# The window-attention stage written out without a loop, its context transposes moved from its first steps to its last, and the expert weights of a routed layer prepared by GpSimd alone

## The reference, cut to what matters

```python
x = x + L0_xattn(layernorm(x), ctx, ...)     # 64 channels, 8 heads of 8, sliding window of 16 along the 512 positions
x = x + L0_ffn(layernorm(x), Wg, Wu, Wd, ...)
x = x + L1_xattn(layernorm(x), ctx, ctx, pos, mask, Wq, Wk, Wv, Wo)     # 32 heads, 8 key heads, width 128
logits = x_norm @ gate_w                      # L1_ffn: routed, 8 experts, the best 2 of each token
w = softmax(top2(logits))
x = x + sum over the 2 experts of w * (x_norm @ expert_w[e])
```

## Time and profile before

| | us |
|---|---|
| median of 3 runs | 1152.22 |
| lowest, highest of them | 1150.52, 1155.11 |
| the profiled execution, its own time | 1149.5 |
| its span in the trace | 1147.7 |
| busy within the span: PE, DVE, POOL, ACT | 1034.4, 662.4, 486.7, 391.5 |

### The profile page before, as it was taken

How to read it: one execution, slowest core, us unless ns; L and a number is a source line. 1 busy time by engine, 2 the same in 40 slices (tenths; PEclk the granted TensorE clock), 3 DMA queues, 4 the chain that set the end, 5 groups by cost and what they waited for, 6 DMA issues and landing times. The chain is left out here.

```text
span 1147.7 us, 24031 instructions
## 1 busy us (share of the span) xinstructions
PE 1034.4 (90%) x9074; PEld 853.3 (74%) x9074; DVE 662.4 (58%) x1380; ACT 391.5 (34%) x894; POOL 486.7 (42%) x539
## 2 busy tenths in 40 slices
PE   6787787999999889999999999999999999754894
PEld 3565566788888678888888888888888888533783
DVE  3787786454454576566565666556566565850424
ACT  3776874222222333222222232222222221511431
POOL 0443442341213245445444455544445542134755
PEclk8898999999999979999999999999999999985997
DMA  7000002655543021111101111110010100035778
GB/s 243 12 3 4 3 4 58 238 179 217 183 174 103 19 74 38 47 29 28 56 29 48 29 28 47 34 51 29 28 47 29 37 10 1 0 119 174 252 237 271
DMA packets 51803, 92.08 MB, mean 80 GB/s; under 512 B 10744, under 2 KB 24312, under 8 KB 51256
## 3 DMA queue, kind: packets, MB, share of 16 engines
q1 hardware_dynamic: 42104, 69.13, 19.0%
q10 hardware_dynamic: 6624, 12.06, 3.1%
q0 software_dynamic: 2976, 9.44, 2.5%
HBM read 77.25 MB, written 36.18 MB: 99 GB/s over the span
## 5 line engine op out<-in xcount | busy, mean ns | idle before, releaser
L115 PE MATMUL PS<-NTh,W 128*128 128x256 f32 (+2 forms) x688 | 216.6, 315 | 0.0
L116 PE MATMUL PS<-NTl,W 128*128 128x256 f32 (+2 forms) x688 | 214.1, 311 | 0.4 <-issue 0.2
L117 PE MATMUL PS<-NTh,W 128*128 128x256 f32 (+2 forms) x688 | 213.9, 311 | 0.0
L116 PEld LDWEIGHTS PS<-NTl,W 128*128 128x128 f32 (+1 forms) x688 | 131.4, 191 | 7.6 <-issue 0.8
L117 PEld LDWEIGHTS PS<-NTh,W 128*128 128x128 f32 (+1 forms) x688 | 129.4, 188 | 8.4
L115 PEld LDWEIGHTS PS<-NTh,W 128*128 128x128 f32 (+1 forms) x688 | 129.7, 188 | 7.1
L1437 POOL TENSOR_TENSOR W<-ca_raw,W 128x512 fp32r<-128x512 f32 x64 | 82.7, 1294 | 115.1 <-ACT W L1287 115.1
L1375 DVE TENSOR_REDUCE ca_su<-room 128x4 f32<-128x256 f32 x64 | 26.9, 420 | 155.8 <-ACT room L1303 155.8
L1404 DVE TENSOR_TENSOR room<-PS,ca_sinT 64x512 f32<-64x512 f32 (+1 forms) x192 | 115.0, 599 | 2.6
L115 PE MATMUL PS<-W,ca_aTh 128*128 128x512 f32 x256 | 106.3, 415 | 3.5 <-DVE X L1392 3.5
L1303 ACT ACTIVATE room<-room 128x256 f32<-128x256 f32 x64 | 26.8, 418 | 222.8 <-POOL room L1484 222.8
(11 more groups left out here) (241 smaller groups left out, 2336.5 us busy)
## 6 DMA issues: line engine op xcount, KB each, us to landing
ca_raw<-in_L_Wq SPq DMA_DIRECT2D x32, 256.0 KB, 2.7
ca_raw<-in_L_Wo SPq DMA_DIRECT2D x32, 256.0 KB, 2.6
rf_raw<-in_experts SPq DMA_DIRECT2D x28, 256.0 KB, 4.0
room<-slots ACTq DMA_DIRECT2D x23, 256.0 KB, 3.4
outs<-room ACTq DMA_DIRECT2D x23, 256.0 KB, 3.8
outs<-blank SPq DMA_DIRECT2D x11, 512.0 KB, 9.0
room<-in_L_Wg SPq DMA_DIRECT2D x10, 256.0 KB, 2.7
room<-in_L_Wu SPq DMA_DIRECT2D x10, 256.0 KB, 3.0
```

The source lines that it names most:

```text
L115: nc.tensor.matmul(out, l_hi, r_hi, start=first, stop=False)
L116: nc.tensor.matmul(out, l_hi, r_lo, start=False, stop=False)
L117: return nc.tensor.matmul(out, l_lo, r_hi, start=False, stop=last)
```

## The change

`pipeline` is no longer called in the first stage. Each engine runs `unrolled`, which writes out all steps n = -4 to 37. The context tiles are transposed by a new piece at the end of steps 32 to 35, two tiles in a step, through PSUM banks 0 and 1, in which the scores were. It waits until the scores of all 32 units have been read out. Two waits are added: PE waits itself for the load of the context before the k projection of tile 0 and of tile 2, and ACT waits at n = 0 until its own masked copies of q are done. One wait (`ct_lo` at TT, before the first L471) is dropped. In the last stage ACT no longer makes high parts in its steps 1 to 4; POOL makes those of experts 2 to 7.

```diff
+def unrolled(eng, step, begin, end, body, per):
+    for n in range(begin, end):
+        step(n, n % body, n // per)
...
-    STEPS = (-4, 8, 24, UNITS + 6, 8, UNITS_PER_TILE)
+    STEPS = (-4, UNITS + 6, 8, UNITS_PER_TILE)
...
-        CT = [sh.PS[:, 2, :], sh.PS[:, 3, :]]
+        CT = [sh.PS[:, 0, :], sh.PS[:, 1, :]]
...
+        def context_due(n):
+            first = 2 * (n - UNITS) if isinstance(n, int) else -1
+            return range(first, first + 2) if 0 <= first < TT else ()
...
@@ tensor
                 def project_context(t, which, done):
+                    if isinstance(t, int) and t in (0, FIRST):
+                        pe.wait_ge(ctx_loaded[t], 16)
...
-                    c = n + 4
-                    if isinstance(n, int) and c < TT:
-                        pe.wait_ge(ctx_loaded[c], 16)
-                        if c >= 2:
-                            pe.wait_ge(S["ct_lo"], c - 1)
-                        for k in range(EC):
-                            last = nc.tensor.transpose(CT[c % 2][:, k * P:(k + 1) * P], sh.CTX[:, c, k * P:(k + 1) * P], ident)
-                        last.then_inc(S["ct_tr"], 1)
...
-                        else:
-                            pe.wait_ge(S["ct_lo"], TT)
...
-                pipeline(pe, step, *STEPS)
+                    for c in context_due(n):
+                        if c == 0:
+                            pe.wait_ge(S["keyed"], UNITS)
+                        if c >= 2:
+                            pe.wait_ge(S["ct_lo"], c - 1)
+                        for k in range(EC):
+                            last = nc.tensor.transpose(CT[c % 2][:, k * P:(k + 1) * P], sh.CTX[:, c, k * P:(k + 1) * P], ident)
+                        last.then_inc(S["ct_tr"], 1)
+
+                unrolled(pe, step, *STEPS)
@@ scalar
                         if q == 0:
+                            if isinstance(t, int) and t == 0:
+                                act.wait_ge(S["q_ready"], 1)
                             add_bias(t + 1, 0, "q_mm", qp[:], "q_biased")
@@ routed_ffn, scalar
-                    if 1 <= j <= 4:
-                        expert_high(2 + (j - 1) // 2, range((j - 1) % 2 * 2, (j - 1) % 2 * 2 + 2))
@@ routed_ffn, gpsimd
-                for e in (1, 2, 3):
-                    expert_low(e)
-                for e in range(RING, EXPERTS):
-                    gp.wait_ge(S["planned"], 1)
-                    done = gp.value_load(free_at[0:1, e - RING:e - RING + 1], min_val=1, max_val=SLOT_TILES + 1)
-                    gp.wait_ge(S["d_mm"], done)
-                    gp.sem_inc(S["planned"])
+                expert_low(1)
+                for e in range(2, EXPERTS):
+                    if e >= RING:
+                        gp.wait_ge(S["planned"], 1)
+                        done = gp.value_load(free_at[0:1, e - RING:e - RING + 1], min_val=1, max_val=SLOT_TILES + 1)
+                        gp.wait_ge(S["d_mm"], done)
+                        gp.sem_inc(S["planned"])
                     for p in range(EC):
```

More of the change, by code:

```diff
@@ L565, in step @@
                                                 sh.CTh[:, :, tok].bitcast(F32), ALU.subtract).then_inc(S["ct_lo"], 1)
-                pipeline(vec, step, *STEPS)
+                unrolled(vec, step, *STEPS)
             @block.gpsimd
@@ L596, in step @@
                                                 ALU.mult).then_inc(S["probs"], 1)
-                pipeline(gp, step, *STEPS)
+                unrolled(gp, step, *STEPS)
             @block.scalar
@@ L669, in step @@
                                              ACT.Copy).then_inc(S["ct_hi"], 1)
-                pipeline(act, step, *STEPS)
+                unrolled(act, step, *STEPS)
         return range(min(x.num for x in S.values()), max(x.num for x in S.values()) + 1)
@@ L1667, in _, with expert_high @@
             def _(act):
-                def expert_high(e, chunks=range(EC)):
-                    for p in chunks:
+                def expert_high(e):
+                    for p in range(EC):
                         k = e * EC + p
```

## The result

The change is faster. Its median is 1142.94 us (8 runs, 1138.53 to 1145.68) against 1153.56 for the kernel before (8 runs, 1150.52 to 1157.72): ratio 0.9904, 95% interval 0.9887 to 0.9920. In a later comparison (six runs) it was 0.9911, 0.9886 to 0.9936. The prediction said 1143.7. The profiled execution took 1139.67 us against 1149.5, a difference of 9.8, and its span is 1137.8. The first stage ends 11.4 us earlier (191.33 and 179.92), and 1.5 us of that are lost again behind it.

The account below looks back on a forecast made before the run. PE is busy 1034.4 of 1147.7 us; gains lie where it waits, in the first stage and first routed tiles. Terms -4.6 - 2.4 - 4.7 - 0.9 + 5.1 - 1.0 = -8.5 take 1152.2 to 1143.7 us; range 1136.5 to 1150.

Parts of the forecast that it names:

- rival 4: Start and routed layer: both gains at full size, -9 and -3; sum -12.5 us, 1139.7 us; chance 0.10.
- the sign of being right: End of the first stage: the last addition to X, at 190.98 us before, would come at 183.5.
- Start, -4.6: Up to unit 0's score read-out: without context work DVE reads out at about 27.2 us, not 31.85; -4.6 us.
- rival 1: First 45 us: PE pauses more, stays at half clock, start gives 3 us only; sum -4.5, 1147.7 us; chance 0.20.
- Unit 0 to 4, -2.4: Read-outs of units 0 to 4: half of 6.7 us context work saved, 0.9 lost to the clock; -2.4 us.
- Loop, -4.7 and -0.9: First-stage loop written out: -4.7 us for one branch back, -0.9 us for shorter waits at three tile boundaries.
- Rival 2: First stage: written-out code must be fetched, four PE pauses of 4.7 us; sum +10.3, 1162.5 us; chance 0.06.
- Tail, +5.1: End of first stage: context work adds 3.9 us over three steps, the end moves 191.33 to 196.4; +5.1 us.
- The ring: Last steps of 3.07 us: ACT's two high parts between its output and values copies lengthen each by 1.3 us.
- Routed layer, -1.0: First slot tiles: the wait behind ACT's weight chunks goes, third tile starts 1.1 us earlier, less 0.1; -1.0 us.
- Rival 3: Routed layer: POOL holds DVE's small tables throughout; sum -6.2 us, 1146.0 us; chance 0.12.
- the 3 us that the prediction gave as a sign: PE: no pause of over 3 us with the releaser "issue" if the prediction is right.

Follow-up runs that it names:

- e4: The kernel before with only PE's first-stage steps written out, DVE, ACT and POOL keeping their loop; 1146.80 us, ratio 0.9947.
- e5: The kernel before with DVE, ACT and POOL written out in the first stage and PE keeping its loop; 1152.62 us, ratio 1.0009.
- e10: The change with context work moved within its steps on PE and ACT, not on DVE, and DVE's routing tables spread over three slot tiles; 1137.68 us, ratio 0.9879.
- e3: The kernel before with only the experts' weight part of the change; 1148.05 us, ratio 0.9972.
- e6: The change with the context work moved to other places within the same last steps on PE, ACT and DVE; 1139.00 us, ratio 0.9889.
- e2: The kernel before, loop kept, with only the context transposes moved to steps 32 to 35 and the two added waits; 1146.16 us, ratio 0.9952.
- e9: The kernel before, context tiles left in front, with DVE's statistics of tiles 2 to 7 made earlier and one ACT wait added; 1146.36 us, ratio 0.9973.
- e1: The kernel before with the first stage written out on all four engines and nothing else changed; 1146.42 us, ratio 0.9954.

## Why the prediction was right, and where its steps were off

The sum was -8.5 us. In the first comparison the medians differ by 10.6 and the profiled executions by 9.8, in the second the medians by 10.0. The sign, the places and the size hold; no rival decided it. That the total came so close is in part luck. The first stage gained 11.4 us where the terms that lie in it sum to 7.5: the start with units 0 to 4 gave 8.3, nearer to rival 4's 9 than to the 7.0 taken, and the tail cost 2 less. Then 3.2 us, for which the sum had nothing, went the other way behind it. The last addition to X came at 179.58, below the 183.5 given as the sign of being right. The terms one by one:

- **Start, -4.6: measured -3.8, and -4.0 over all executions.** The mechanism is as said: DVE is no longer late, and ACT's last copy is next. The step that failed is the time of that copy, 24.8 in the prediction and 25.96 in the profile. Of these 1.2, 0.5 were there from the start (the first projection begins at 14.33 in place of 13.84, chance by the other executions; counted from it the term is -4.3); 0.4 are ACT's wait of 0.33 for the v projection at half clock, with the 0.1 by which operations in a row overlap; 0.2 are the two context copies, counted at 0.59 where the next operation had followed at 0.48. The mask and the scores then took 1.8 at half clock, 0.5 more than the prediction's 1.3 and 0.75 more than the 1.08 that they take at full clock (before, from 37.47), but the slack given was larger. So the clock's part, rival 1's mechanism in the place that it named, is 0.4 + 0.75, some 1.2 us, where rival 1 had 4.
- **Unit 0 to 4, -2.4: measured -4.5, and -4.1 over all.** Two parts. The work was put at half of 6.7, which was too little; the clock had the wrong sign. I added 0.9 for a PE that would pause more. In fact before has half clock at 44 to 48, and after full clock from 30 on. The four operations of PE from 43.80 to 49.04 before take 1.9 us longer than the same ones in after at full clock (L378 2.05 for 1.13, L426 0.77 for 0.49, L433 1.10 for 0.67, L471 1.09 for 0.85), and that is about the most that the clock gave: the other half clock of before in these steps, at 32 to 36 (0.61 and 0.54), has its like in after at 28 to 30. In e4, with the context tiles in place, PE has full clock from 40 us on, and unit 0 to 4 takes 15.64 against 16.04 to 16.53 in the other four, so there it was worth 0.4 to 0.9. The rest of the 4.1 is DVE's and ACT's work and waits. Before, PE fell at 42 to 44 behind 2.1 us of idle time that the context tiles caused; without the delay there was no such pause. By these rows the delays, not the transposes, set the clock here; no run took out one without the other.
- **Loop, -4.7 and -0.9: measured -6.0, and -5.7 over all.** Right in mechanism, and by e4 and e5 narrower than stated: PE's branch alone, with the transfer of code in its pause. The Trainium skill's page "Runtime: NRT & Kernel Launch" (section "Instruction fetch mechanics") holds that straight code is fetched ahead and that a taken branch can make the engine wait for its code. The trace agrees, with the transfer of 16 KB in the pause of 3.60. Rival 2 (pauses of 4.7 us in the written-out code) did not come: the longest pause of that kind in the first stage is 0.9. Why three engines pass their branch without a loss no run here shows. Nor was it tested that a constant in place of a register is what shortens the other boundaries (2.19 and 1.87).
- **Tail, +5.1: measured +3.1.** The ring was placed rightly for n = 33 and 34, +1.1 and +1.2 against 1.3. The step that failed is the third: it gave n = 35 the same 1.3, but the values' last copy (unit 31, on ACT at 171.42) is made in the step before, so in that step ACT's high parts stand in front of nothing that PE's next product by the values needs. It grew by 0.2, and the end by 0.6 where 1.2 was placed. That the place of the work costs, and not its amount, is shown by e10: with the same work, 1.9 us of the 3.1 are gone, 1.4 of them in the two long steps and 0.6 at the end. PE's wait of 1.00 for ACT's copy of the values names ACT's high parts as the reason; but e10 moves PE's transposes along with them, and no run moves one alone.
- **Routed layer, -1.0: measured -1.7, and -1.6 in e3.** The first wait went as placed (0.9 less). The third also went, because DVE's tables happened to miss POOL's batches. The same code took 23.6 to 23.8 us in three executions and 26.2 in e6, so the term is a matter of phase, and over the four it is -1.2 against the mean of 25.5 of the six executions with the old experts' part and tables. Rival 3 is thus true as a mechanism, POOL's casts included, but it cost PE more than before in one execution of four, and there by another price than was given: 1.0 in the wait, and 1.6 by the half clock behind it. The Trainium skill's page "SBUF — State Buffer" (section "Who interferes with whom") says that DVE's copy, cast and tensor_scalar can be shut out by GpSimd too, and not only two-input operations, but reductions not; the trace agrees for three of them: the cast 1.16 and the scalar operation 1.23 in place of 0.17, the reduction to 128x6 elements 0.20 in either case.
- **What was given back later.** The prediction had nothing between the first stage and slot tile 0, and the profile has +1.3; behind slot tile 6 it has +1.9. The last is chance: 70.5 to 73.2 us over all fourteen executions, with means of 71.7 and 71.9 without and with the experts' part. About half of it goes with PE's pause at the last slot tile: the mean is 72.3 in the seven executions that have it and 71.3 in the seven that don't. This pause of 3.19 with "issue" is over the 3 us that the prediction gave as a sign, but in another stage than its branch. The +1.3 is not so plain. That stretch takes 860.0 to 862.2, mean 860.8, in the five executions in which PE has its loop (before, e2, e3, e5, e9), and 861.5 to 866.3, mean 863.3, in the nine in which PE's code is written out. Of the 2.5, 2.4 lie between the ends of PE's work in the second and the third stage, whose code is the same, and about half is to be seen there as pauses of PE with the releaser "issue" (2.2 us in all on average, against 3.4). A cost of the longer program on PE outside of its own stage fits, but the run that varies PE's code alone does not show it: e4 has 861.5, inside the range of the five, and its median lies 5.0 us below that of before, against 5.7 in its units 8 to 24. e1, with all four engines written out, has 864.9, and 5.3 against 6.1. So at most a small part of the loop's gain was given back in those two, and where the 2.5 come from stays open.

Put together from means over the executions, with the start counted from the first projection: -4.3 - 4.1 - 5.7 + 3.1 - 1.2 + 2.5 = -9.7, against 10.6 and 10.0 measured.

## What to carry to other kernels

When side work is taken off a start-up chain, look for every queue that it stood in (here ACT's copies, DVE's order and through it PE's projection), and read the clock of both profiles stretch by stretch: here the work that filled gaps went with full clock at 20 to 24 us, and the pause of 2.1 us that its delays made at 42 with half clock behind it. A ring of engines pays only for what stands between two links of it, so the same 1.2 us of ACT cost 1.1 in two steps and 0.2 in the third, and could be moved to a place where they cost little, provided that no release of a buffer stands behind them. Small operations of DVE beside long ones of GpSimd are a matter of phase: spread them, so that none is on the way of the next tile. And count a wait of the matmul engine with what comes behind it: 2.14 us of waiting cost 1.6 more at half clock, 1.10 us cost nothing more.

## What was not expected of the hardware

- One taken branch of PE costs 3.6 to 4.1 us of idle time and the half clock of what follows, 5.7 us of the stage on average with the other boundaries, and the idle time is a transfer of 16 KB of code (1.00 to 1.41) plus 2.6 us in each of five executions; the branches of DVE, ACT and POOL at the same step cost nothing that can be measured (e5, ratio 1.0009).
- An operation of DVE on 128x6 elements takes 0.17 us alone and up to 1.23 beside a batch of POOL's 128x512 subtractions; one on 128x8 takes 0.60 beside a cast of 0.61.
- Two executions of programs with the same routed layer differ by 2.5 us in its first seven tiles, by where POOL's batch stands when DVE comes; over half of this is PE's half clock behind the longer wait.
